# Graph attention kernel: placement one-hots built one group ahead, aggregation put first in TensorE's group

## The chip, the cores and the metric

One NeuronCore of one Trainium2 chip. The metric is the device time of one execution in microseconds (us), as the median of the runs shown; lower is better.

## What is computed

The reference is one transformer-like layer over a graph: x becomes x + GNN(norm x) + linear attention(norm x), and then x + mixture of experts(norm x), for 3125 nodes of 256 features. The part around the change is the graph attention over 53125 edges, which come sorted by their target:

```python
mod_k = K[src] + 0.2 * rel_w[edge_relations][:, None, :]
scores = jnp.einsum('ehd,ehd->eh', Q[dst], mod_k) / D ** 0.5      # 4 heads of 64
ex = jnp.exp(scores - segment_max(scores, dst)[dst])
w = ex / segment_sum(ex, dst)[dst]
agg = segment_sum(w[:, :, None] * V[src], dst)
```

Everything else (layer norms, projections, linear attention, top-2 routing and experts) is untouched.

## The kernel before, in words

The kernel runs in phases: projections (to about 205 us), edges (`phase_edges`, about 205 to 884 us), combination, routing, experts, end. Only the edge phase concerns us.

Edges are handled in blocks of 128. A step is two blocks (256 edges) that all point into one block of 128 nodes; the code numbers steps by p. A group, numbered `G_`, is 4 blocks, so two steps, and a chunk, numbered c, is 4 groups (g = 0 to 3). There are 29 chunks and 116 groups. Every engine has its own list of instructions, written out in Python in the order in which it runs; semaphores tie the lists together, and nothing reorders them.

All engines walk through rounds i = 0 to 30 of four groups. In round i three chunks are in work at once:

- chunk i is **scored**. POOL (GpSimd) has gathered the rows of K and V of its edges into the ring `KV` with one indirect DMA for each block (L572). VectorE compares the edge's target and relation with an iota to make the one-hots `PT` and `OT` of the group after (`onehots`, L743 and L744). TensorE multiplies them with the relation table (`relations`, into `ps_u`) and the queries (`queries`, one for each step, into `ps_qe`). VectorE adds `ps_u` to K (`modify`, L754), multiplies by `ps_qe` (`multiply`, L761, one for each step) and sums over a head (`reduce`, L767).
- chunk i-1 goes through the **softmax**: the scores are turned on TensorE (`turn_scores` in g = 0, `turn_ends` in g = 1, `turn_carries` in g = 2, `turn_weights` in g = 3) and VectorE runs the segment maxima in between: `run_forward` and `run_backward` (SF, SB) in g = 0, `carry` and `carried` (EC, EZ, CR) in g = 1, two `carry_in` and `differences` (SM, SD) in g = 2, `first_rows` and `factors` (OH, LR) in g = 3.
- chunk i-2 is **summed**. ScalarE weighs the V rows (`weigh`, L587; in the last two chunks VectorE does every other step). VectorE makes the placement one-hots `PM` of a whole group (`place`, L772): `PM[edge, node] = (iota == DC[edge])`. TensorE multiplies the weighed V rows by `PM` (`aggregate`, L677) and adds the block's old sums (`add_sums`, L683), and ScalarE copies the result back into `ACC` (`keep_sums`, L595).

`PM` has two buffers, and `place(p)` waits until the `aggregate` two groups back is done (`s_pw`); `aggregate(p)` waits for `s_pm` (the placement) and `s_wv` (the weighed rows). In VectorE's group the order is: one-hots of the next group, `modify`, `place`, first `multiply`, second `multiply`, `reduce`, with the softmax instructions strewn in. In TensorE's group it is: a turn of the softmax, `relations`, `add_sums(p-1)`, `queries`, `aggregate(p)`, `add_sums(p)`, `queries`, (`turn_weights`), `aggregate(p+1)`.

Of the kernel before, what the change touches and what calls it, by code (L numbers as in the profile page):

```python
# [74 lines left out]
def wait(eng, sem, count):  # L75

    if isinstance(count, int) and count <= 0:
        return
    eng.wait_ge(sem, count)
# [8 lines left out]
def load_values(nc, engine, ap, high):  # L88

    return nc.values_load_multi_w_load_instructions(ap, engines=(engine,), min_val=0, max_val=high,  # L90
                                                    skip_runtime_bounds_check_because="the step list holds node blocks only")[1]
# [421 lines left out]
def phase_edges(nc, sem, T, d):  # L513
# [9 lines left out]
    NG = NCH * CG  # L523
    NP = NCH * CP
# [6 lines left out]
    def on_vector(p):  # L531
        return p >= VP and p % 2 == 1
# [4 lines left out]
    with nc.Block() as block:  # L537
# [103 lines left out]
        @block.tensor  # L641
        def _(pe):
            def relations(G_):
                h = G_ % 2
                pe.wait_ge(s_oh, 2 * G_ + 2)
                wait(pe, s_ku, G_ - 1)
                for k in range(G):
                    for n in range(3):
                        m = pe.matmul(T["ps_u"][:, h, k * D:(k + 1) * D], T["OT"][:, h, k * P:(k + 1) * P], T["rel3"][:, n, :],  # L649
                                      start=(n == 0), stop=(n == 2))  # L650
                m.then_inc(s_u, 1)

            def queries(p, at):
                h = p // 2 % 2
                wait(pe, s_mu, p - 2)
                for k in range(2):
                    for n in range(3):
                        m = pe.matmul(T["ps_qe"][:, p % 3, k, :], T["PT"][:, h, (p % 2 * 2 + k) * P:(p % 2 * 2 + k + 1) * P],  # L658
                                      T["Q3"][:, bass.ds(at + n * C, C)], start=(n == 0), stop=(n == 2))
                m.then_inc(s_qe, 1)  # L660

            def rows(G_):
                return load_values(nc, mybir.EngineType.PE, T["qRow"][0:1, 2 * G_:2 * G_ + 2], (NT - 1) * 3 * C)

            def blocks(p):
                return load_values(nc, mybir.EngineType.PE, T["aRow"][0:1, p:p + 2], (NT - 1) * A)

            def aggregate(p):
                c, x = divmod(p, CP)
                pe.wait_ge(s_pm, p // 2 + 1)  # L670
                if on_vector(p):
                    pe.wait_ge(s_wd, (p - VP) // 2 + 1)
                else:
                    pe.wait_ge(s_wv, p + 1 if p < VP else VP + (p - VP) // 2 + 1)
                wait(pe, s_acc, p - 1)
                for k in range(2):
                    m = pe.matmul(T["ps_o"][:, p % 2, 0:A], PM[:, p // 2 % 2, p % 2 * 2 + k, :], kv[:, c % KR, 2 * x + k, C:KVW], start=(k == 0), stop=False)  # L677
                m.then_inc(s_pw, 1)

            def add_sums(p, at):  # L680
                wait(pe, s_acc, p)
                pe.wait_ge(s_rs, p // CP + 1)
                pe.matmul(T["ps_o"][:, p % 2, 0:A], T["ident"][:, :], ACC[:, bass.ds(at, A)], start=False, stop=True).then_inc(s_o, 1)  # L683

            def turn_scores(c):
                pe.wait_ge(s_sc, (c + 1) * CG)
                wait(pe, s_w, 2 * c)
                pe.transpose(ps_s[0:B, 0:P], S[:, c % 2, :], T["ident"][:, :]).then_inc(s_t1, 1)

            def turn_ends(c):  # L690
                pe.wait_ge(s_sm, c * SMV + 2)
                pe.transpose(ps_s[0:1, P:P + B], T["SB"][:, P - 1:P], T["ident"][0:B, 0:B])
                pe.transpose(ps_s[0:1, P + B:P + 2 * B], T["SB"][:, 0:1], T["ident"][0:B, 0:B]).then_inc(s_t2, 1)

            def turn_carries(c):
                pe.wait_ge(s_sm, c * SMV + 7)
                pe.transpose(ps_s[0:B, 256:257], T["CR"][0:1, 0, :], T["ident"][0:1, 0:1])
                pe.transpose(ps_s[0:B, 257:258], T["CR"][0:1, 1, :], T["ident"][0:1, 0:1]).then_inc(s_t3, 1)

            def turn_weights(c):  # L700
                pe.wait_ge(s_ex, c + 1)
                pe.transpose(ps_s[:, 264:264 + B], T["SE"][:, 0:P], T["ident"][0:B, 0:B])
                pe.wait_ge(s_lr, c + 1)
                pe.matmul(ps_s[:, 258:258 + H], T["LR"][:, :], T["ident"][0:H, 0:H], start=True, stop=True).then_inc(s_t4, 1)
            at = rows(0)
            relations(0)
            queries(0, at[0])
            queries(1, at[1])
            for i in range(NCH + 2):
                for g in range(CG):  # L710
                    p = (i - 2) * CP + 2 * g
                    G_ = i * CG + g + 1
                    if 1 <= i <= NCH:
                        (turn_scores, turn_ends, turn_carries, lambda c: None)[g](i - 1)
                    if G_ < NG:
                        at = rows(G_)
                        relations(G_)
                    if p >= 1:
                        add_sums(p - 1, before)
                    if G_ < NG:  # L720
                        queries(2 * G_, at[0])
                    if p >= 0:
                        to = blocks(p)
                        aggregate(p)
                        add_sums(p, to[0])
                        before = to[1]
                    if G_ < NG:
                        queries(2 * G_ + 1, at[1])
                    if 1 <= i <= NCH and g == 3:
                        turn_weights(i - 1)  # L730
                    if p >= 0:
                        aggregate(p + 1)
            add_sums(NP - 1, before)

        @block.vector
        def _(v):
# [26 lines left out]
            def reduce(G_):  # L763
                c, g = divmod(G_, CG)
                v.wait_ge(s_mu, 2 * G_ + 2)
                wait(v, s_t1, c - 1)
                v.tensor_reduce(S[:, c % 2, g * G * H:(g + 1) * G * H].rearrange("p (s h) -> p s h", h=H),  # L767
                                keys(G_).rearrange("p s (h d) -> p s h d", h=H), AX.X, ALU.add).then_inc(s_sc, 1)

            def place(p):  # L770
                wait(v, s_pw, p - 2)
                v.tensor_tensor(PM[:, p // 2 % 2, :, :], T["iota_f"][:, :].unsqueeze(1).broadcast_to([P, G, P]),  # L772
                                T["DC"][:, 2 * p:2 * p + G].unsqueeze(2).broadcast_to([P, G, P]), ALU.is_equal).then_inc(s_pm, 1)
# [81 lines left out]
            for i in range(NCH + 2):  # L855
                for g in range(CG):
                    G_ = i * CG + g
                    p = (i - 2) * CP + 2 * g
                    c = i - 1
                    scored, softmax, summed = G_ < NG, 1 <= i <= NCH, i >= 2  # L860
                    if G_ + 1 < NG:
                        onehots(G_ + 1)
                    if softmax and g == 3:
                        first_rows(c)
                    if scored:
                        modify(G_)
                    if softmax and g == 2:
                        carry_in(c, 0)
                    if softmax and g == 3:
                        factors(c)  # L870
                    if summed:
                        place(p)
                    if softmax and g == 0:
                        run_forward(c)
                    if softmax and g == 2:
                        carry_in(c, 1)
                    if scored:
                        multiply(2 * G_)
                    if softmax and g == 2:
                        differences(c)  # L880
                    if summed and on_vector(p + 1):
                        weigh(p + 1)
                    if scored:
                        multiply(2 * G_ + 1)
                    if summed and g == 0:
                        rescale(i - 2)
                    if softmax and g == 0:
                        run_backward(c)
                    if softmax and g == 1:
                        carry(c)  # L890
                    if scored:
                        reduce(G_)
                    if softmax and g == 1:
                        carried(c)

# [776 lines left out]
```

## Time and profile before

| | us |
|---|---|
| median of 3 runs (1359.99 to 1361.61) | 1360.5 |
| the profiled execution, its own time | 1360.95 |
| its span in the profile | 1359.1 |
| VectorE (DVE) busy over the span | 939.8 (69%) |
| TensorE (PE) busy | 1123.6 (83%) |
| ScalarE (ACT) busy | 816.7 (60%) |
| POOL busy | 776.2 (57%) |

The shares are averages over all phases and say little about one of them. How to read it: first the table by stretches of the edge phase (how busy each engine is there), then the table of waits (who stands still, and for whom), then the timeline of single instructions. A record of an instruction often starts some 0.07 us before its forerunner's ends, so what an instruction costs is the distance from its start to the next one's start, not its duration.

### The profile page before, as it was taken

Reading aid. Unit: us, or ns where it says so; the run is one execution under the profiler, and the core shown is the slowest. Engines: PE = TensorE matmul, PEld = TensorE weight load, DVE = VectorE, ACT = ScalarE, POOL = GpSimd, SP = SyncE. Lnnn points to the kernel's source line nnn. Section 1 sums busy time; section 2 is a strip of 40 time slices with the busy share of each in tenths; the row PEclk is TensorE's granted clock in tenths of the full one; section 3 lists DMA queues with packets and bytes.
Section 4 is the critical chain, followed back from the end, with each engine's and each line's share of the span. In section 5 each row is a group of like instructions: output and inputs, shape, how many; then the busy total and the mean of one; then the engine's idle time right before and its main releaser. Section 6 shows DMA issues by size and latency. Waiting matters only on the chain. (4 is left out here: it accounts for less than half of the span.)

```text
span 1359.1 us, 26561 instructions
## 1 busy us (share of the span) xinstructions
PE 1123.6 (83%) x7285; PEld 867.0 (64%) x7286; DVE 939.8 (69%) x2100; ACT 816.7 (60%) x2868; POOL 776.2 (57%) x853
## 2 busy tenths in 40 slices
PE   5999926899999999999999998756775589999950
PEld 3777724566666666666666666545653379999940
DVE  7676327999999999999999999346563812122215
ACT  3444300588888888888888888512342066776630
POOL 4666347777777777777777774033220644554520
PEclk9999966799999999999999999989985789999985
DMA  7332358888788888878778775092101822221218
GB/s 224 114 104 98 109 111 254 237 236 230 234 227 235 227 236 233 232 231 231 231 232 233 229 234 155 0 328 81 39 20 61 257 59 70 66 69 66 69 37 281
DMA packets 132710, 225.06 MB, mean 166 GB/s; under 512 B 23555, under 2 KB 89098, under 8 KB 132594
## 3 DMA queue, kind: packets, MB, share of 16 engines
q0 software_dynamic: 43456, 138.49, 34.9%
q1 hardware_dynamic: 89138, 85.16, 20.7%
q8 instruction: 56, 0.92, 0.3%
q14 instruction: 60, 0.49, 0.1%
HBM read 191.18 MB, written 32.40 MB: 165 GB/s over the span
## 5 line engine op out<-in xcount | busy, mean ns | idle before, releaser
L572 POOL DMA_INDIRECT KV<-kv,ixs x464 | 494.4, 1065 | 142.6 <-issue 139.6
L587 ACT ACTIVATE KV<-KV,WS 128x65 f32<-128x65 f32 x1792 | 453.6, 337 | 22.5 <-ACT RR L613 17.0
L677 PE MATMUL ps_o<-KV,PM 128*128 128x260 f32 x928 | 256.2, 399 | 25.8 <-DVE PM L772 12.8
L677 PEld LDWEIGHTS ps_o<-KV,PM 128*128 128x128 f32 x928 | 158.7, 190 | 73.8 <-DVE PM L772 29.5
L658 PE MATMUL ps_qe<-Q,PT 128*128 x1392 | 199.6, 282 | 5.2 <-DVE KV L761 5.2
L658 PEld LDWEIGHTS ps_qe<-Q,PT 128*128 128x128 bf16 x1392 | 138.7, 100 | 55.2 <-issue 8.5
L683 PE MATMUL ps_o<-ACC,ident 128*128 x464 | 154.2, 414 | 0.0
L761 DVE TENSOR_TENSOR KV<-KV,ps_qe 128x512 f32<-128x512 f32 x232 | 148.4, 667 | 0.2
L754 DVE TENSOR_TENSOR KV<-KV,ps_u 128x1024 f32<-128x1024 f32 x116 | 139.6, 1204 | 6.9 <-DMA KV<-kv,ixs 6.9
L1491 DVE TENSOR_TENSOR YG<-ps_y,B 128x256 f32<-128x256 f32 x56 | 23.8, 425 | 170.1 <-PE ps_y L1465 170.1
L767 DVE TENSOR_REDUCE S<-KV 128x16 f32<-128x1024 f32 x116 | 139.4, 1202 | 2.0
L595 ACT COPY ACC<-ps_o 128x260 f32 x232 | 85.0, 366 | 55.7 <-PE ps_o L683 54.8
L1408 ACT ACTIVATE HT<-ps_h,WB 128x128 f32<-128x128 f32 x224 | 82.2, 367 | 60.2 <-PE ps_h L1449 47.2
L1449 PE MATMUL ps_h<-XT,WB 128*128 128x128 f32 x896 | 115.2, 282 | 0.0
L1449 PEld LDWEIGHTS ps_h<-XT,WB 128*128 128x128 f32 x896 | 105.7, 194 | 5.3 <-issue 2.2
L1379 POOL DMA_INDIRECT ytab<-YG,DX x56 | 55.3, 987 | 93.2 <-issue 83.4
L1465 PE MATMUL ps_y<-W,HT 128*128 x448 | 105.8, 380 | 0.0
L683 PEld LDWEIGHTS ps_o<-ACC,ident 128*128 128x128 f32 x464 | 76.8, 189 | 21.1 <-issue 9.3
L649 PE MATMUL ps_u<-rel,OT 64*128 64x64 bf16 x1392 | 62.0, 194 | 32.3 <-DVE OT L744 29.3
L649 PEld LDWEIGHTS ps_u<-rel,OT 64*128 64x128 bf16 x1392 | 50.6, 97 | 56.5 <-DVE OT L744 45.3
L1465 PEld LDWEIGHTS ps_y<-W,HT 128*128 128x128 f32 x448 | 81.0, 191 | 8.6
L772 DVE TENSOR_TENSOR PM<-iota_f,DC 128x512 f32<-128x512 f32 x116 | 78.1, 674 | 3.7 <-PE ps_o L677 3.7
(300 smaller groups left out, 1685.3 us busy)
## 6 DMA issues: line engine op xcount, KB each, us to landing
dlb<-dl_rows SPq DMA_DIRECT2D x116, 128.0 KB
W<-in_f_W_dram SPq DMA_DIRECT2D x16, 512.0 KB, 6.2
tyb<-ty_rows SPq DMA_DIRECT2D x116, 64.0 KB
KV<-kv,ixs POOLq DMA_INDIRECT x464, 4.3
kv<-kvb SPq DMA_DIRECT2D x25, 258.0 KB, 2.3
xs_rows<-xs SPq DMA_DIRECT2D x25, 256.0 KB, 2.4
YF<-ytab SPq DMA_DIRECT2D x8, 640.0 KB, 9.2
VB<-kv SPq DMA_DIRECT2D x5, 650.0 KB, 9.1
```

Source lines behind the costliest of these rows:

```text
L572: pool.indirect_dma_start(kv[:, c % KR, n, :], None, d["kv"], bass.IndirectOffsetOnAxis(ap=T["ixs"][:, c % KR, n:n + 1], axis=0)).then_inc ...
L587: m = a.activation(part, part, ACT.Copy, scale=W[:, c % 2, s * H + h:s * H + h + 1])
L595: a.copy(ACC[:, bass.ds(at, A)], T["ps_o"][:, p % 2, 0:A]).then_inc(s_acc, 1)
L649: m = pe.matmul(T["ps_u"][:, h, k * D:(k + 1) * D], T["OT"][:, h, k * P:(k + 1) * P], T["rel3"][:, n, :], start=(n == 0), stop=(n == 2))
L658: m = pe.matmul(T["ps_qe"][:, p % 3, k, :], T["PT"][:, h, (p % 2 * 2 + k) * P:(p % 2 * 2 + k + 1) * P], T["Q3"][:, bass.ds(at + n * C, C)] ...
L677: m = pe.matmul(T["ps_o"][:, p % 2, 0:A], PM[:, p // 2 % 2, p % 2 * 2 + k, :], kv[:, c % KR, 2 * x + k, C:KVW], start=(k == 0), stop=False)
L683: pe.matmul(T["ps_o"][:, p % 2, 0:A], T["ident"][:, :], ACC[:, bass.ds(at, A)], start=False, stop=True).then_inc(s_o, 1)
L754: v.tensor_tensor(k, k, T["ps_u"][:, G_ % 2, 0:G * D].rearrange("p (s d) -> p s d", s=G).unsqueeze(2).broadcast_to([P, G, H, D]), ALU.add) ...
L761: v.tensor_tensor(k, k, T["ps_qe"][:, p % 3, :, :], ALU.mult).then_inc(s_mu, 1)
L767: v.tensor_reduce(S[:, c % 2, g * G * H:(g + 1) * G * H].rearrange("p (s h) -> p s h", h=H), keys(G_).rearrange("p s (h d) -> p s h d", h= ...
L1449: r = pe.matmul(T["ps_h"][:, m, 0:SLOTS], WB[:, u % 2, k * HID + m * P:k * HID + (m + 1) * P], XT[:, u % 2, k, :], start=(k == 0), stop=(k ...
L1465: r = pe.matmul(T["ps_y2"][:, (u % YB) * HB + w, 0:C], HT[:, u % 2, m, w * P:(w + 1) * P], T["W2"][:, bass.ds(at + m * C, C)], start=(m == ...
```

## The change

`place` moves from the middle of VectorE's group, where it made the placements of the step pair p in the group in which they are used, to the end of the group before. It now follows `reduce`, and comes ahead of `carried` in g = 1 and ahead of the next group's `onehots`. On TensorE the group now begins (after the softmax turn) with `add_sums(p-1)` and `aggregate(p)`; `relations` and the first `queries` come behind them, then `add_sums(p)`, `aggregate(p+1)`, and the second `queries` last. No instruction is added or removed, and buffers stay as they are.

```diff
                         (turn_scores, turn_ends, turn_carries, lambda c: None)[g](i - 1)
+                    if p >= 1:
+                        add_sums(p - 1, before)
+                    if p >= 0:
+                        to = blocks(p)
+                        aggregate(p)
                     if G_ < NG:
                         at = rows(G_)
                         relations(G_)
-                    if p >= 1:
-                        add_sums(p - 1, before)
-                    if G_ < NG:
                         queries(2 * G_, at[0])
                     if p >= 0:
-                        to = blocks(p)
-                        aggregate(p)
                         add_sums(p, to[0])
                         before = to[1]
-                    if G_ < NG:
-                        queries(2 * G_ + 1, at[1])
                     if 1 <= i <= NCH and g == 3:
                         turn_weights(i - 1)
                     if p >= 0:
                         aggregate(p + 1)
+                    if G_ < NG:
+                        queries(2 * G_ + 1, at[1])
...
                         factors(c)
-                    if summed:
-                        place(p)
                     if softmax and g == 0:
...
                         reduce(G_)
+                    if -2 <= p < NP - 2:
+                        place(p + 2)
                     if softmax and g == 1:
                         carried(c)
```

VectorE, from `modify` of g = 1 to the next group's one-hots, in a middle round. Before:

```order
L754 TENSOR_TENSOR KV<-KV,ps_u 128x4x256
L772 TENSOR_TENSOR PM<-iota_f,DC 128x512
L761 TENSOR_TENSOR KV<-KV,ps_qe 128x2x256 x2
L816 SCALAR_TENSOR_TENSOR EC<-ET,EZ 1x72
L817 SCALAR_TENSOR_TENSOR EC<-ET,EZ 1x72
L767 TENSOR_REDUCE S<-KV 128x16
L824 COPY EZ<-EC 1x4
L825 TENSOR_TENSOR CR<-EC,ET 1x4x16
L826 TENSOR_TENSOR CR<-EC,ET 1x4x16
L743 TENSOR_SCALAR PT<-dlb,iota_p 128x512
L744 TENSOR_SCALAR OT<-tyb,iota_p 64x512
```

and the same engine with the change, from the same `multiply` on, into g = 2:

```order
L761 TENSOR_TENSOR KV<-KV,ps_qe 128x2x256 x2
L816 SCALAR_TENSOR_TENSOR EC<-ET,EZ 1x72
L817 SCALAR_TENSOR_TENSOR EC<-ET,EZ 1x72
L767 TENSOR_REDUCE S<-KV 128x16
L772 TENSOR_TENSOR PM<-iota_f,DC 128x512
L824 COPY EZ<-EC 1x4
L825 TENSOR_TENSOR CR<-EC,ET 1x4x16
L826 TENSOR_TENSOR CR<-EC,ET 1x4x16
L743 TENSOR_SCALAR PT<-dlb,iota_p 128x512
L744 TENSOR_SCALAR OT<-tyb,iota_p 64x512
L754 TENSOR_TENSOR KV<-KV,ps_u 128x4x256
L835 SCALAR_TENSOR_TENSOR SM<-BR,ps_s,SB 64x128
```

The placement no longer stands between L754 and L761, and it now stands shortly ahead of the one-hots L743 and L744 (next to them in every group but this one, where `carried` lies between).

TensorE, the group g = 1 of a middle round (L649 relations, L658 queries, L677 aggregate, L683 add_sums). Before:

```order
L649 MATMUL ps_u<-rel,OT 128x64 x12
L683 ISA
L683 MATMUL ps_o<-ACC,ident 128x260
L658 ISA
L658 MATMUL ps_qe<-Q,PT 128x256
L658 ISA
L658 MATMUL ps_qe<-Q,PT 128x256
L658 ISA
L658 MATMUL ps_qe<-Q,PT 128x256 x4
L90 TENSOR_LOAD aRow
L677 MATMUL ps_o<-KV,PM 128x260 x2
```

and with the change:

```order
L692 MATMUL ps_s<-ident,SB 1x64
L693 MATMUL ps_s<-ident,SB 1x64
L683 ISA
L683 MATMUL ps_o<-ACC,ident 128x260
L90 TENSOR_LOAD aRow
L677 MATMUL ps_o<-KV,PM 128x260 x2
L90 TENSOR_LOAD qRow
L649 MATMUL ps_u<-rel,OT 128x64 x12
```

The work that needs the fresh one-hots `OT` now stands behind an `add_sums` and an `aggregate` that need nothing made in VectorE's same group.

## Rows read from the trace of the kernel before

**Rows 1.** Table by stretches, 500 to 600 us; the header names the columns

```profile
core 0: us, PE busy (x) PEld busy (x) DVE busy (x) ACT busy (x) POOL busy (x), PEclk, DMA share, GB/s
500.00:600.00 100.00, 94.21 (x691) 68.53 (x690) 99.69 (x195) 87.28 (x353) 77.75 (x74) 1.00 0.82 232
```

**Rows 2.** Table of waits, TensorE, 300 to 820 us: us in total, times, longest

```profile
PE ps_u L649 <- DVE OT L744: 15.0, 33, 0.6
PE ps_o L677 <- DVE PM L772: 8.6, 23, 0.4
```

**Rows 3.** Timeline, VectorE, the target one-hots PT; start, us, engine, line, operation

```profile
521.72 0.49 DVE L743 TENSOR_SCALAR PT<-dlb,iota_p 128x512 bf16<-128x512 bf16 x1
...
527.24 0.41 DVE L743 TENSOR_SCALAR PT<-dlb,iota_p 128x512 bf16<-128x512 bf16 x1
...
532.79 0.56 DVE L743 TENSOR_SCALAR PT<-dlb,iota_p 128x512 bf16<-128x512 bf16 x1
...
538.16 0.35 DVE L743 TENSOR_SCALAR PT<-dlb,iota_p 128x512 bf16<-128x512 bf16 x1
...
543.78 0.49 DVE L743 TENSOR_SCALAR PT<-dlb,iota_p 128x512 bf16<-128x512 bf16 x1
```

**Rows 4.** Timeline, VectorE: modify ahead of multiply, and modify ahead of the placement

```profile
234.83 1.22 DVE L754 TENSOR_TENSOR KV<-KV,ps_u 128x1024 f32<-128x1024 f32 x1 [0.17 <-DMA KV<-kv,ixs]
236.09 1.29 DVE L761 TENSOR_TENSOR KV<-KV,ps_qe 128x512 f32<-128x512 f32 x2
...
256.29 1.20 DVE L754 TENSOR_TENSOR KV<-KV,ps_u 128x1024 f32<-128x1024 f32 x1
257.42 0.67 DVE L772 TENSOR_TENSOR PM<-iota_f,DC 128x512 f32<-128x512 f32 x1
```

**Rows 5.** Timeline, VectorE, group 6: the two carry_in with nothing between

```profile
241.33 0.34 DVE L835 SCALAR_TENSOR_TENSOR SM<-BR,ps_s,SB 64x128 f32<-64x128 bf16 x1
241.71 0.35 DVE L835 SCALAR_TENSOR_TENSOR SM<-BR,ps_s,SM 64x128 f32<-64x128 bf16 x1
241.98 0.67 DVE L761 TENSOR_TENSOR KV<-KV,ps_qe 128x512 f32<-128x512 f32 x1
```

**Rows 6.** Timeline, POOL and VectorE: one-hots that start inside a gather

```profile
289.38 0.95 POOL L572 DMA_INDIRECT KV<-kv,ixs  x1 [0.31 <-issue]
...
289.88 0.57 DVE L743 TENSOR_SCALAR PT<-dlb,iota_p 128x512 bf16<-128x512 bf16 x1
```

**Rows 7.** Timeline, POOL: a gather that starts inside the placement at 257.42

```profile
257.50 1.43 POOL L572 DMA_INDIRECT KV<-kv,ixs  x1 [0.31 <-DVE KV L754]
```

**Rows 8.** Timeline, VectorE and POOL: a gather that starts inside CR, PT and OT behind

```profile
261.71 0.25 DVE L826 TENSOR_TENSOR CR<-EC,ET 1x64 f32<-1x64 f32 x1
261.85 0.33 DVE L743 TENSOR_SCALAR PT<-dlb,iota_p 128x512 bf16<-128x512 bf16 x1
262.11 0.34 DVE L744 TENSOR_SCALAR OT<-tyb,iota_p 64x512 bf16<-64x512 bf16 x1
...
261.75 1.53 POOL L572 DMA_INDIRECT KV<-kv,ixs  x1 [0.30 <-issue]
```

**Rows 9.** Timeline: last gather of a group and the modify that reads it, early and in the middle

```profile
245.92 0.95 POOL L572 DMA_INDIRECT KV<-kv,ixs  x1 [0.30 <-issue]
...
250.74 1.22 DVE L754 TENSOR_TENSOR KV<-KV,ps_u 128x1024 f32<-128x1024 f32 x1 [0.38 <-DMA KV<-kv,ixs]
...
516.12 0.95 POOL L572 DMA_INDIRECT KV<-kv,ixs  x1 [0.30 <-issue]
...
522.39 1.20 DVE L754 TENSOR_TENSOR KV<-KV,ps_u 128x1024 f32<-128x1024 f32 x1
```

**Rows 10.** Timeline, TensorE: relations and queries of one group

```profile
517.72 0.51 PE L649 MATMUL ps_u<-rel,OT 64*128 64x64 bf16 x12
...
518.70 0.82 PE L658 MATMUL ps_qe<-Q,PT 128*128 x6
```

**Rows 11.** Timeline, TensorE, the last scored group's first aggregate

```profile
844.31 1.14 PE L677 MATMUL ps_o<-KV,PM 128*128 128x260 f32 x4 [1.60 <-DVE PM L772]
```

## The prediction

> **What bounds the kernel now.** I read three views, in this order. First the table by stretches [rows 1]: in the middle of the edge phase VectorE is busy 99.69 of 100 us, TensorE 94.21, ScalarE 87.28, POOL 77.75, and the granted clock is 1.00, the upper of TensorE's two levels, so no clock is to be won. Then the table of waits [rows 2]: TensorE does wait for what the change touches, 15.0 us for the relation one-hots and 8.6 us for the placements in 520 us, together nearly 1.0 us in each of the 23.5 chunks that fit there. That is what the new order removes. But a wait on an engine that is not the last one costs nothing, and VectorE has no row of waiting at all in that stretch. So the third view is the timeline of VectorE, start to start: a chunk takes 22.06 us, from the one-hots at 521.72 to the same ones at 543.78 [rows 3]. TensorE's 23.6 us are therefore no term of the sum. Only what shortens or lengthens VectorE's own chunk is.
>
> **What the change does to VectorE's chunk.** The same instructions run; their neighbours change, and that has a price in three places.
>
> One. In g = 1 the placement stood between `modify` and the first `multiply`, which reads what `modify` wrote. Where the two stood next to each other, the starts are 236.09 - 234.83 = 1.26 us apart; with the placement behind `modify` they are 257.42 - 256.29 = 1.13 [rows 4]. The cover goes, and 0.13 us is added. In g = 0 and g = 3 a softmax instruction (SF, LR) is left between, in g = 2 two of them, so nothing is added there.
>
> Two. In g = 2 the placement stood between the two `carry_in`, of which the second reads the first. Side by side they start 0.38 us apart, while the one after follows its forerunner, on which it doesn't depend, after 0.27 [rows 5]: 0.11 us added. Together 0.24 us a chunk.
>
> Three, a gain that the diff doesn't show. The one-hots PT last 0.49, 0.41, 0.56 and 0.35 us in the four groups of a chunk [rows 3], the same from chunk to chunk. The shortest is 0.35 and early rows go to 0.33; I take 0.34 as the work itself, and (0.15 + 0.07 + 0.22 + 0.01) = 0.45 us a chunk as time lost. The loss has a place: PT starts 0.50 us into a gather of POOL and ends 0.12 after it, 290.45 against 290.33 [rows 6]. POOL loses by VectorE too: the gather that starts at 257.50 inside the placement (257.42 to 258.09) lasts 1.43 us instead of 0.95 [rows 7], that is, it ends 0.84 after the placement, as if begun 0.11 before its end. The closest picture of the new order is the one where POOL's gather begins inside CR and the two one-hots follow closely [rows 8]: there PT and OT run at 0.33 and 0.34, unstretched, and it is the gather that waits until OT's end (262.45 + 0.83 = 263.28, its end). With the change every pair of one-hots comes behind a placement, which like CR reads two tensors of SBUF. POOL needs 4 x (0.95 + 0.30) = 5.0 us for a group and VectorE 5.5, so POOL gains on VectorE in every group until a placement catches it; then PT runs free. So I take the whole 0.45 as won. Bounds of this term: 0 (POOL stays in a phase where PT starts half-way into a gather) and 0.45, and I stand at the upper end since the rows that look like the new order are [rows 8].
>
> The sum for a chunk is 0.13 + 0.11 - 0.45 = -0.21 us, so 21.85 for 22.06. Placement and softmax both run in 27 rounds; the first of them still waits for gathers, so 26 count: -5.5 us.
>
> The Trainium skill, "SBUF — State Buffer", section "SBUF: two separate sides", has a rule for this: VectorE and GpSimd share one pair of ports as an exclusive lock, and whoever starts first holds it for its whole instruction. For the stretched PT the trace agrees (0.57 us, ended by the gather's end). By the letter of it a gather under way would hold the one-hots for up to 0.95 us in the new order as well, and a chunk could lose the 0.45 again or more. This rule speaks against the gain, and is the ground of rival B below.
>
> **TensorE and ScalarE.** TensorE's group loses its waits for OT and PM, together 1.0 us a chunk, all of it slack. A new wait can arise in g = 0: `aggregate` needs rows that ScalarE can only weigh once the softmax weights have come from `turn_weights`, and relations (0.51) and queries (0.82) [rows 10] no longer stand between. That is at most 1.3 us a chunk. The cover is TensorE's idle time, 5.8 us in 100 [rows 1], so 1.3 us a chunk; I cost it at nothing, and at 0 to 0.3 if the cover is short. What is queued behind this wait is the next relations and queries. VectorE needs those only in its next group: relations ready at 518.23 are read by the `modify` at 522.39, and queries ready at 519.52 by the `multiply` 1.13 us behind it [rows 4, 9, 10], so each may be 4 us late for free, more than the `aggregate` and `add_sums` that they now stand behind and the new wait make together. The second `queries`, now last in the group, are needed one `multiply` later still. SP's loads of the next rows hang on the one-hots, which keep their place in the group. Each `place` runs one group earlier and waits for an `aggregate` of the group before, done by then. POOL's queue has nothing moved.
>
> **The ends.** In the last scored group TensorE stands 1.60 us for the placement [rows 11]; the new order has it ready. Between 0 and 1.60 us can be won; ScalarE is weighing the rows for the same product at that time, so I take 0.4. After that, weighing paces everything and the order is as before. Early, the first placement falls into a group end followed by a wait for gathers (0.38 us before the `modify` at 250.74 [rows 9]); I take 0.
>
> Total -5.9 us on the profiled execution's own 1360.95, so 1355.1; the median of the runs is 0.45 lower, and the forecast is **1355** us in round numbers. What a measurement of this kernel can tell from no change is about 0.2%, 2.7 us.
>
> **Rivals.**
>
> A, slower: the gathers become the bound. A placement alone holds a gather to about 0.1 us before its own end; with PT and OT behind it, the hold reaches from the placement's start over PM 0.60 (0.67 less the overlap of 0.07), PT 0.26 and OT 0.34, less 0.12: 1.1 us [rows 7, 8], more in g = 1 and g = 2, where CR and OH join the row; I take 1.2. POOL's group is then 5.0 plus a hold of 0 to 1.2 us. As long as the mean hold is below 5.5 - 5.0 = 0.45, VectorE sets the pace; above it, VectorE waits in `modify`. For a random phase the mean is 0.6, a group 5.6, a chunk 22.5 or 0.45 more than now: +12 us, 1373. If each gather is caught at the placement's start, a group is 6.2 and 104 groups add 80 us. For it: the hold is twice as long as now, and the reserve is small: a gather's landing takes 250.74 - 246.87 = 3.9 us after its record ends, and the lead in the middle is 522.39 - 517.07 = 5.3 [rows 9], 1.4 us to spare. Against it: a lead, once there, grows whenever VectorE is the slower of the two, and then POOL is only held for the difference. Chance 0.17.
>
> B, slower: a gather that began just before the placement holds the one-hots behind it, as in [rows 6], and the stretch of PT stays at its 0.45 in another phase. It decides if POOL's gather has passed its start before VectorE's placement takes the memory. The sum becomes +0.24 x 26 = +6.2, less 0.4: 1367. Chance 0.09.
>
> C, no change: a third to half of the 0.45 stays, or TensorE's new wait in g = 0 eats 0.1 to 0.2 us of each chunk. -0.05 a chunk, 1359. Chance 0.20.
>
> D, faster by far: VectorE's 99.7% hides waits inside its records, and TensorE's 1.0 us of waiting a chunk is really on the path: -26 us, 1335. Against it stands that VectorE's steps add up to its chunk with nothing left over. Chance 0.03.
>
> My forecast has 0.51. Its own range is 1349 (both dependence costs absent, the gain whole: -0.45 x 26 = -11.7) to 1358. The range for everything must leave out no more than 2 in 10: it goes from 1349 up to 1373, over B and to A's middle value, and leaves out D and the worse half of A. Faster is the forecast and D, 0.54; within 0.2% is C, 0.20; slower are A and B, 0.26.
>
> **What would show it.** Right: PT near 0.34 us in all four groups; the start of `modify` to that of `multiply` 1.26 in g = 1 and the two `carry_in` 0.38 apart; no row of TensorE waiting for PM, hardly one for OT; gathers of more than 1 us, ended by OT's end, about one a group; a chunk of 21.85. Wrong: `modify` with idle time ended by the gathers (rival A), PT still at 0.4 to 0.6 (B), `multiply` waiting for `ps_qe` or SF for `turn_scores` (TensorE became late, C).

## The result and the profile after

| | before | with the change |
|---|---|---|
| median of 4 runs each, us | 1360.24 (1359.47 to 1361.61) | 1387.72 (1386.67 to 1389.86) |
| ratio, 95% interval | | 1.0203 [1.0185, 1.0221] |
| span of the profiled execution, us | 1359.1 | 1384.9 |

The change makes the kernel 2.0% slower, 27.5 us. The forecast was 1355, its range ended at 1373, and most of the chance stood on faster. Both the sign and the range were wrong.

The same three views, in the same order. First the table by stretches of the kernel with the change, 500 to 600 us (columns as in [rows 1]):

```profile
500.00:600.00 100.00, 88.45 (x653) 63.56 (x651) 93.91 (x179) 82.49 (x334) 71.77 (x69) 1.00 0.78 220
```

Every engine is less busy than in [rows 1]: VectorE 93.91 for 99.69, TensorE 88.45 for 94.21. The granted clock is 1.00 as before. When all engines lose share together, no single one of them has become the bound; they wait for each other in turn. Then the table of waits, 300 to 820 us (us in total, times, longest):

```profile
PE ps_o L677 <- issue: 58.3, 89, 1.2
ACT ACC L595 <- PE ps_o L683: 57.7, 76, 1.1
POOL KV L572 <- PE ps_o L683: 46.4, 46, 1.7
DVE SF L805 <- PE ps_s L688: 24.7, 22, 1.5
```

The two rows of [rows 2] are gone, as foreseen. In their place TensorE stands 58.3 us ahead of `aggregate` (L677), 89 times, which is once in every group, and 58.3 / 520 x 23.12 = 2.6 us a chunk. ScalarE stands 57.7 us ahead of `keep_sums` (L595) for `add_sums` (L683); the kernel before has the same row, but shorter:

```profile
ACT ACC L595 <- PE ps_o L683: 35.8, 88, 0.6
```

VectorE, which had no waiting row, stands 24.7 us in `run_forward` (SF) for the turned scores (L688), 1.1 us in each of 22 chunks. "issue" ahead of L677 means that the view found no releaser; the timeline below shows that `weigh` (L587) ends just before.

VectorE's own instructions did what the forecast said. Its timeline with the change:

```profile
452.41 0.35 DVE L743 TENSOR_SCALAR PT<-dlb,iota_p 128x512 bf16<-128x512 bf16 x1
453.13 1.20 DVE L754 TENSOR_TENSOR KV<-KV,ps_u 128x1024 f32<-128x1024 f32 x1
...
457.56 0.35 DVE L743 TENSOR_SCALAR PT<-dlb,iota_p 128x512 bf16<-128x512 bf16 x1
...
460.39 0.41 DVE L805 TENSOR_TENSOR_SCAN SF<-BR,ps_s 64x128 f32<-64x128 bf16 x1 [1.10 <-PE ps_s L688]
...
464.35 0.34 DVE L743 TENSOR_SCALAR PT<-dlb,iota_p 128x512 bf16<-128x512 bf16 x1
464.87 1.20 DVE L754 TENSOR_TENSOR KV<-KV,ps_u 128x1024 f32<-128x1024 f32 x1
466.11 1.28 DVE L761 TENSOR_TENSOR KV<-KV,ps_qe 128x512 f32<-128x512 f32 x2
...
469.87 0.34 DVE L743 TENSOR_SCALAR PT<-dlb,iota_p 128x512 bf16<-128x512 bf16 x1
...
476.25 1.20 DVE L754 TENSOR_TENSOR KV<-KV,ps_u 128x1024 f32<-128x1024 f32 x1
```

PT lasts 0.34 to 0.35 in all four groups, where [rows 3] has 0.35 to 0.56, and `modify` to `multiply` in g = 1 is 466.11 - 464.87 = 1.24. Yet the chunk is 476.25 - 453.13 = 23.12 us for 22.06: the 1.10 of waiting stands in the middle of it. Of 23.12 us VectorE is idle (100 - 93.91)% = 1.41, so its work is 21.71, a little less than the 21.85 that I forecast for a chunk without waits. The loss, 1.06 us a chunk by 26 = 27.6 us, is all waiting.

Where the wait comes from is seen when one follows a single step around TensorE and ScalarE. The timeline with the change, from the `aggregate` of step p to that of step p+2, with the `aggregate` of step p-2 on top:

```profile
455.16 1.12 PE L677 MATMUL ps_o<-KV,PM 128*128 128x260 f32 x4 [0.93 <-issue]
...
461.46 1.11 PE L677 MATMUL ps_o<-KV,PM 128*128 128x260 f32 x4 [0.74 <-issue]
...
462.51 0.52 PE L649 MATMUL ps_u<-rel,OT 64*128 64x64 bf16 x12
462.96 0.83 PE L658 MATMUL ps_qe<-Q,PT 128*128 x6
463.63 0.60 PE L683 MATMUL ps_o<-ACC,ident 128*128 x2
...
464.35 0.38 ACT L595 COPY ACC<-ps_o 128x260 f32 x1 [0.80 <-PE ps_o L683]
...
464.90 2.03 ACT L587 ACTIVATE KV<-KV,WS 128x65 f32<-128x65 f32 x8 [0.18 <-issue]
...
467.03 1.11 PE L677 MATMUL ps_o<-KV,PM 128*128 128x260 f32 x4 [0.43 <-issue]
...
472.62 1.11 PE L677 MATMUL ps_o<-KV,PM 128*128 128x260 f32 x4 [0.50 <-issue]
```

and in the kernel before:

```profile
519.56 1.11 PE L677 MATMUL ps_o<-KV,PM 128*128 128x260 f32 x4
...
520.60 0.70 PE L683 MATMUL ps_o<-ACC,ident 128*128 x2
...
521.55 0.36 ACT L595 COPY ACC<-ps_o 128x260 f32 x1
...
521.96 2.03 ACT L587 ACTIVATE KV<-KV,WS 128x65 f32<-128x65 f32 x8
...
524.54 1.04 PE L677 MATMUL ps_o<-KV,PM 128*128 128x260 f32 x4
```

It is a ring: `aggregate(p)`, `add_sums(p)`, `keep_sums(p)`, then `weigh(p+2)`, which stands behind `keep_sums(p)` in ScalarE's list, then `aggregate(p+2)`. Before, `add_sums` starts 1.04 us behind `aggregate`, and there is slack at the ring's end: `weigh` ends at 523.99, and `aggregate` starts 0.55 us later, behind TensorE's other work. Now `relations` and the first `queries` of the next group are between `aggregate` and `add_sums`, which starts 2.17 us behind. A round takes 467.03 - 461.46 = 5.57 us, 472.62 - 467.03 = 5.59, and the one from g = 3 to g = 0, in which `turn_weights` and the copies of WS and RR stand as well, 6.30 (455.16 to 461.46). The last `aggregate` of the chunk, at 478.29, follows 5.67 behind 472.62. That the four rounds make 23.13 us, a chunk, proves nothing by itself: four rounds of any list do. What counts is that nowhere in this ring is there slack: in all four rounds each link starts at most 0.6 us behind the end of its forerunner, on whichever engine that is, and none of its links waits for VectorE. In the round from g = 3 to g = 0 two ways end together, `keep_sums` at 458.43 and `turn_weights` at 458.45, and ScalarE's copy of WS starts at 458.48; that round would hardly be shorter with `add_sums` further ahead, the other three would. The place where VectorE pays is SF: TensorE works without a pause from the `aggregate` at 455.16, which the ring holds back, through the second `queries`, now ahead of `turn_scores`, to the end of `turn_scores` at 460.28, and SF starts at 460.39.

### The profile page after: what moved, and what is told of

Same layout as the page of the kernel before. It is cut to its first block and busy times, and to the rows that moved or that the text cites. A ratio compares the mean times of both kernels' runs of the same rounds, so it can differ in the third digit from the quotient of the medians.

```text
span 1384.9 us, 26561 instructions
## 1 busy us (share of the span) xinstructions
PE 1111.8 (80%) x7285; PEld 855.1 (62%) x7286; DVE 938.0 (68%) x2100; ACT 817.2 (59%) x2868; POOL 764.4 (55%) x853
## 5 line engine op out<-in xcount | busy, mean ns | idle before, releaser
L572 POOL DMA_INDIRECT KV<-kv,ixs x464 | 480.9, 1036 | 180.1 <-issue 128.2
L587 ACT ACTIVATE KV<-KV,WS 128x65 f32<-128x65 f32 x1792 | 453.7, 336 | 28.1 <-ACT RR L613 16.9
L677 PE MATMUL ps_o<-KV,PM 128*128 128x260 f32 x928 | 253.8, 396 | 82.6 <-issue 74.0
L677 PEld LDWEIGHTS ps_o<-KV,PM 128*128 128x128 f32 x928 | 165.0, 190 | 145.8 <-issue 123.0
L658 PE MATMUL ps_qe<-Q,PT 128*128 x1392 | 200.2, 283 | 3.6 <-DVE KV L761 3.6
L658 PEld LDWEIGHTS ps_qe<-Q,PT 128*128 128x128 bf16 x1392 | 129.9, 100 | 42.1 <-issue 6.1
L761 DVE TENSOR_TENSOR KV<-KV,ps_qe 128x512 f32<-128x512 f32 x232 | 149.1, 671 | 1.8 <-PE ps_qe L658 0.6
L683 PE MATMUL ps_o<-ACC,ident 128*128 x464 | 146.3, 397 | 0.0
L754 DVE TENSOR_TENSOR KV<-KV,ps_u 128x1024 f32<-128x1024 f32 x116 | 139.7, 1204 | 4.6 <-DMA KV<-kv,ixs 4.5
L595 ACT COPY ACC<-ps_o 128x260 f32 x232 | 84.6, 364 | 97.3 <-PE ps_o L683 85.4
L649 PEld LDWEIGHTS ps_u<-rel,OT 64*128 64x128 bf16 x1392 | 48.9, 97 | 53.2 <-issue 36.9
L683 PEld LDWEIGHTS ps_o<-ACC,ident 128*128 128x128 f32 x464 | 70.6, 191 | 7.2 <-issue 0.6
L649 PE MATMUL ps_u<-rel,OT 64*128 64x64 bf16 x1392 | 62.9, 194 | 13.9 <-DVE OT L744 13.9
```

Source lines behind the costliest of these rows:

```text
L572: pool.indirect_dma_start(kv[:, c % KR, n, :], None, d["kv"], bass.IndirectOffsetOnAxis(ap=T["ixs"][:, c % KR, n:n + 1], axis=0)).then_inc ...
L587: m = a.activation(part, part, ACT.Copy, scale=W[:, c % 2, s * H + h:s * H + h + 1])
L595: a.copy(ACC[:, bass.ds(at, A)], T["ps_o"][:, p % 2, 0:A]).then_inc(s_acc, 1)
L754: v.tensor_tensor(k, k, T["ps_u"][:, G_ % 2, 0:G * D].rearrange("p (s d) -> p s d", s=G).unsqueeze(2).broadcast_to([P, G, H, D]), ALU.add) ...
L761: v.tensor_tensor(k, k, T["ps_qe"][:, p % 3, :, :], ALU.mult).then_inc(s_mu, 1)
```

## Experiments

The theory, **ring**: the loss comes from what stands between `aggregate(p)` and `add_sums(p)`, and goes with its length. Rivals: the placement's new place (beside the one-hots and POOL's gathers) costs; or it costs as such that TensorE's work for VectorE stands behind an `aggregate`.

The 18 runs fell into two kinds of sessions. In one, the kernel before took 1361 us, as in the result. In the others it took 1468 to 1481, and ratios there are measured against that. The expectations call it another kind of chip; but the recorded chip number is the same for one session at 1481 and for the one at 1361, so whether it is the chip is not known. The granted clock differs too: over 300 to 820 us it is 1.00 in every profile of the 1361-us kind (before, after, before_q, v_sh40), and in the other 0.98 for the kernel before, 0.90 to 0.92 for VectorE's part alone, and 0.86 to 0.89 for sums_next3, rel_between and the full change.

### VectorE's part alone: v_only, and again

```diff
-                    if summed:
-                        place(p)
...
                         reduce(G_)
+                    if -2 <= p < NP - 2:
+                        place(p + 2)
```

TensorE's list is that of the kernel before.

> VectorE's part alone: place one group ahead and behind reduce; TensorE's order as before. Theory 1 (the slowdown is a ring between TensorE and ScalarE that only TensorE's new order makes: aggregate, relations and queries, add_sums, keep_sums, weigh, aggregate two steps on): this kernel has no such ring, VectorE sets the pace, PT lasts 0.34 us in every group, a chunk takes 21.85 us and the kernel 1354 to 1356. Theory 2 (the placement ahead of the one-hots is what costs, through POOL's gathers or VectorE's own steps): most of the 27 us is here, 1375 or more, with modify waiting for gathers.

> VectorE's part alone. Theory 1: a chunk of 21.85 us, PT 0.34 us in every group, 1354 to 1356 where the kernel before takes 1360. Theory 2: 1375 or more, with modify waiting for gathers.

> VectorE's part alone, TensorE's list as in the kernel before. Theory ring and port gain: on a chip where the kernel before takes 1360 about 1355; on one where it takes 1475 again 1.045. Rival (the placement at the group's end has a price of its own on every chip): 1.02 or more on the first kind of chip too.

Measured: 1538.64 us, 1.046 [1.043, 1.049]; 1536.80, 1.042 [1.036, 1.047]; 1534.42, 1.041 [1.035, 1.048], all in sessions of the second kind (1475-us sessions from here on). The forecast for it was missed: a clear loss where none, or a gain, was expected. What it is made of is taken up below, with its counterpart in a 1361-us session.

### TensorE's part alone: t_only, and the placement in its old spot

t_only is the change with `place(p)` back where it was; ahead_mid has `place(p + 2)`, one group ahead as in the change, but in the old spot between `modify` and `multiply`.

> TensorE's part alone: its new order, with place in its old spot, made in the group that uses it. Theory 1: the ring is whole, 1386 to 1392, no faster than the full change; a placement that is ready only some 1.8 us behind modify is about as late as the weighed rows. Theory 2: about 1360, since the placement is where it was.

> The full change, but place(p + 2) stands between factors and run_forward or multiply, its old spot in the group, still a group ahead. Theory 1: VectorE isn't the bound, so its neighbours don't matter: 1385 to 1390, as the full change. Theory 2 (placement, one-hots and gathers in a row are the cost): the row is broken up, so back to 1360 or less.

Measured: t_only 1606.06, 1.092 [1.088, 1.095]; ahead_mid 1609.28, 1.093 [1.088, 1.098]. The full change in such sessions is 1.096 to 1.100 (below). So where `place` stands makes little difference once TensorE has its new order; TensorE's order carries the large part.

### add_sums directly behind aggregate: sums_next, four times

```diff
                         aggregate(p)
+                        add_sums(p, to[0])
+                        before = to[1]
                     if G_ < NG:
                         at = rows(G_)
                         relations(G_)
                         queries(2 * G_, at[0])
-                    if p >= 0:
-                        add_sums(p, to[0])
-                        before = to[1]
```

Everything else is the full change, the `aggregate` ahead of `relations` included.

> The full change, but add_sums(p) directly behind aggregate(p), ahead of relations and queries. Theory 1: relations and queries (1.1 us from start to start) leave the ring, which falls from 5.6 to about 4.5 us a group, below VectorE's 5.46; a chunk is 21.85 to 22.0 and the kernel 1354 to 1358. If only the hand-over of the softmax weights in g = 0 were the cause (6.3 us in that group), it would stay above 1375: the path from turn_weights to the first aggregate is unchanged.

> The full change with add_sums(p) directly behind aggregate(p). Theory 1: the ring falls from 5.6 to about 4.5 us a group, below VectorE's 5.46, and the kernel takes 1354 to 1358 where the kernel before takes 1360. If only the hand-over of the softmax weights in g = 0 were the cause, it stays above 1375.

> The full change with add_sums(p) directly behind aggregate(p). Theory ring: the 1.0 us a chunk that the change loses on the first chip is gone, so on a chip where the kernel before takes 1360 about 1355 (0.995 to 1.00); on one where it takes 1475, 1540 as before (1.045). Rival (the placement at the group's end has a price of its own on every chip): 1.02 or more on the first kind of chip too.

> The full change with add_sums(p) directly behind aggregate(p). If this is a chip where the kernel before takes 1360: theory ring, the time of VectorE's part alone, 0.990 to 1.000 (a chunk of 21.8 to 22.0 us, VectorE over 99% busy). Rival (TensorE's new order costs as such, with relations and queries behind an aggregate): 1.01 or more. If it takes 1475: 1.045 as before.

Measured, all in 1475-us sessions: 1540.98, 1539.79, 1544.30 and 1540.35 us, ratios 1.048, 1.043, 1.046 and 1.046 (the widest interval 1.037 to 1.052). It is within 0.7% of the time of v_only in the same sessions. So there, that `relations` and `queries` stand behind an `aggregate` costs next to nothing; that they stand ahead of `add_sums` costs 5%. The clock does not make that difference, since sums_next3 and full3 both have 0.86. One caution: these kernels do not stand still alike (below). VectorE waits 58.9 us in `modify` for something outside the core in sums_next3, 40.7 in full3 and not at all in v_only3, in 300 to 820 us, so the near equality with v_only may in part be chance.

### The full change on the same ground, and the kernel before

> The full change once more, beside the kernel before on one chip, since the first four kernels ran where the kernel before itself took 1470 us and ScalarE stood for 4 to 6 us at a time on something that came from outside the core. Theory 1 (the ring between TensorE and ScalarE): 1385 to 1390 where the kernel before takes 1360; every chunk 23.1 us; VectorE waits 1.1 us a chunk for turn_scores. Theory 2 (placement beside the one-hots): the same time.

> The full change again, beside the other three on the same chip: 1388 (1.02) on a chip where the kernel before takes 1360, 1615 (1.09) where it takes 1475. It is the mark that tells which of the two kinds of chip these four ran on.

> The kernel before, unchanged, for its profile on the chip where it takes 1476 us. If ScalarE's standstills of 5 to 6 us, ended from outside the core, are the chip's and not the change's, they are here too, about one in 29 us, and the chunk takes some 26 us instead of 22.1. If they belong to the new orders, ScalarE has none of them here and something else makes the 1476.

Measured: full2 1621.18, 1.096 [1.089, 1.104]; full3 1620.70, 1.100 [1.094, 1.105]; before_here 1489.07 beside 1480.83 for the same kernel, one execution each.

### Half of it between them: rel_between, twice

```diff
                         relations(G_)
-                        queries(2 * G_, at[0])
                     if p >= 0:
                         add_sums(p, to[0])
                         before = to[1]
+                    if G_ < NG:
+                        queries(2 * G_, at[0])
```

> The full change, but of the two pieces that it put between aggregate(p) and add_sums(p) only relations stays there; the first queries comes behind add_sums(p). Theory ring (what lies between the two lengthens aggregate -> add_sums -> keep_sums -> weigh -> next aggregate by its own time): relations is 0.45 us of the 1.2, so the ring of 5.58 us becomes about 4.8 within a chunk and 5.5 from g = 3 to g = 0, below or at VectorE's 5.4 a group, so the time is that of sums_next. On a chip where the kernel before takes 1360: about 1355, ratio 1.00; on one where it takes 1475: a ratio of 1.04 to 1.05. Rival: it is enough that TensorE's work for VectorE stands behind an aggregate, whatever is between aggregate and add_sums: then as the full change, 1388 (1.02) or 1610 (1.09).

> relations alone between aggregate(p) and add_sums(p), the first queries behind. If this is a chip where the kernel before takes 1360: theory ring, the four rings of a chunk are 0.82 us shorter each than in the full change, 3.3 us of its 23.1, so VectorE bounds again: 0.990 to 1.003. Rival (it is enough that they stand behind an aggregate): 1.02. If it takes 1475: 1.065 as before.

Measured: 1580.23, 1.065 [1.054, 1.076], and 1572.41, 1.072 [1.068, 1.076]. Neither the time of sums_next, which I expected since the ring should have fallen below VectorE's pace, nor that of the full change, which the rival wanted: it lies half-way. The dose shows in the waits as well. TensorE ahead of `aggregate`, 300 to 820 us, in sums_next3:

```profile
PE ps_o L677 <- issue: 13.1, 23, 1.5
PE ps_o L677 <- ACT KV L587: 1.6, 1, 1.6
```

in rel_between:

```profile
PE ps_o L677 <- issue: 22.3, 32, 1.6
PE ps_o L677 <- ACT KV L587: 20.6, 15, 1.6
```

and in full3:

```profile
PE ps_o L677 <- ACT KV L587: 41.9, 28, 1.7
PE ps_o L677 <- issue: 26.3, 28, 1.6
```

14.7, 42.9 and 68.2 us in the same stretch, with nothing, with `relations`, and with `relations` and `queries` between `aggregate` and `add_sums`; the median chunk, from `modify` to `modify`, is 28.6, 29.8 and 31.2 us. In these sessions the time grows with what stands between the two, and from the first piece on. Why the ring costs more there than in the others (5%, where the full change is 2.6% above v_sh40 in the other kind) is not shown; one reading is that the rounds are stretched by stalls from outside (below) and have no slack to give.

### Only the ring, in the kernel before: before_q

```diff
-                    if G_ < NG:
-                        queries(2 * G_, at[0])
                     if p >= 0:
                         to = blocks(p)
                         aggregate(p)
+                    if G_ < NG:
+                        queries(2 * G_, at[0])
+                    if p >= 0:
                         add_sums(p, to[0])
```

> The kernel before with one piece moved: the first queries of a group goes from ahead of aggregate(p) to between aggregate(p) and add_sums(p). Theory ring: the way aggregate -> add_sums -> keep_sums -> weigh -> aggregate becomes 0.8 us longer and nothing else changes, so the kernel gets slower by what rel_between and full3 differ by on this chip, 1.02 to 1.04. Rival (the loss comes from relations and queries being late for VectorE, or from add_sums(p-1) and aggregate(p) standing ahead of them): 1.00, since in this kernel they stand where they stood or 1.1 us later.

Measured, in the 1361-us session: 1371.10 for 1361.05, 1.007 [1.005, 1.009]. The sign is the one expected; the size, taken from the other sessions, was too large. The timeline from g = 3 to g = 0:

```profile
541.16 1.14 PE L677 MATMUL ps_o<-KV,PM 128*128 128x260 f32 x4 [1.03 <-DVE PM L773]
...
542.79 0.60 PE L683 MATMUL ps_o<-ACC,ident 128*128 x2
...
543.51 0.38 ACT L595 COPY ACC<-ps_o 128x260 f32 x1 [0.97 <-PE ps_o L683]
...
544.19 0.38 PE L704 MATMUL ps_s<-ident,LR 4*128 4x4 f32 x2
...
544.61 0.21 ACT L612 COPY WS<-ps_s 128x64 f32<-128x64 f32 x1 [0.71 <-PE ps_s L704]
...
545.46 2.03 ACT L587 ACTIVATE KV<-KV,WS 128x65 f32<-128x65 f32 x8 [0.58 <-ACT RR L613]
...
547.59 0.68 PE L677 MATMUL ps_o<-KV,PM 128*128 128x260 f32 x2 [0.70 <-ACT KV L587]
...
547.95 0.43 DVE L788 SCALAR_TENSOR_TENSOR ACC<-RR,ACC 128x260 f32 x1 [0.51 <-ACT ACC L595]
```

This round is 6.43 us, and the chunk 22.60 (from the `aggregate` at 524.99 to that at 547.59), 0.5 more than before. One piece out of two gives a third of the full loss. But the rows show another way than the ring. `keep_sums` ends at 543.89, and ScalarE's copy of WS starts 0.72 us later, for `turn_weights` (L704): the way over `add_sums` and `keep_sums` has slack in this round. What is late is `turn_weights`. `aggregate`, moved up by a `queries`, first waits 1.03 us for the placement, since this kernel makes it in the same group, and the `queries` and all behind it start that much later. VectorE pays at `rescale` (L788), which waits for ScalarE's `keep_sums`, 0.5 us a chunk (11.6 us, 24 times), the whole difference. This loop, from `place` over TensorE and ScalarE back to `rescale`, runs through VectorE; the ring of the full change does not. So before_q shows that TensorE's order alone can cost VectorE time by way of ScalarE, and is no test of the ring.

### VectorE's part in the 1361-us session: v_sh40, v_sh80, before_sh40

```diff
+            for n in range(40):
+                a.copy(T["pad"][:, n:n + 1], T["SRC"][:, 0:1])
             for i in range(NCH + 2):
```

These add 40 (in v_sh80 80) tiny copies to ScalarE's list, ahead of its first `weigh`, where it is idle; v_sh40 and v_sh80 are v_only with them, before_sh40 the kernel before with them. They were meant to move the stalls that ScalarE shows in the 1475-us sessions.

> The kernel before with 40 tiny copies (128 x 1, into a tile nobody reads) added to ScalarE's list at a time when it is idle, ahead of its first weigh. Theory L (the stalls of ScalarE on this chip come with the place in its own list of instructions): they move to other groups of the chunk and the time changes, by up to 3% in either direction. Theory D (they come with what the DMA engines carry at that time): nothing moves, 1.00.

> v_only3 with the same 40 copies. Theory L: the one stall of 5.5 us a chunk leaves the place just ahead of exponents, and the ratio leaves 1.041, down to between 0.99 and 1.03. Theory D: 1.041 again, stall in the same place.

> v_only3 with 80 copies. Theory L: a ratio that differs from that of v_sh40 and of v_only3. Theory D: 1.041 again.

Measured: before_sh40 1360.14, 0.9997 [0.9986, 1.0008]; v_sh40 1351.98, 0.9941 [0.9922, 0.9961]; v_sh80 1351.41, 0.9925 [0.9901, 0.9949]. There were no such stalls when these ran, so about them the three say nothing. They say something better: the copies cost nothing, so v_sh40 and v_sh80 are a clean measurement of VectorE's part, a gain of 8 to 10 us. The rows of v_sh40 (here L745 is PT, L756 `modify`, L837 `carry_in`):

```profile
500.00:600.00 100.00, 93.92 (x694) 69.27 (x693) 99.35 (x195) 85.89 (x353) 74.68 (x75) 1.00 0.83 237
```

```profile
502.05 0.33 DVE L745 TENSOR_SCALAR PT<-dlb,iota_p 128x512 bf16<-128x512 bf16 x1
502.57 1.20 DVE L756 TENSOR_TENSOR KV<-KV,ps_u 128x1024 f32<-128x1024 f32 x1
503.71 0.34 DVE L837 SCALAR_TENSOR_TENSOR SM<-BR,ps_s,SB 64x128 f32<-64x128 bf16 x1
504.08 0.35 DVE L837 SCALAR_TENSOR_TENSOR SM<-BR,ps_s,SM 64x128 f32<-64x128 bf16 x1
...
507.65 0.35 DVE L745 TENSOR_SCALAR PT<-dlb,iota_p 128x512 bf16<-128x512 bf16 x1
...
512.80 0.35 DVE L745 TENSOR_SCALAR PT<-dlb,iota_p 128x512 bf16<-128x512 bf16 x1
...
518.38 0.34 DVE L745 TENSOR_SCALAR PT<-dlb,iota_p 128x512 bf16<-128x512 bf16 x1
...
524.38 1.20 DVE L756 TENSOR_TENSOR KV<-KV,ps_u 128x1024 f32<-128x1024 f32 x1
```

The chunk is 524.38 - 502.57 = 21.81 us; the forecast said 21.85. VectorE is busy 99.35 of 100 us, PT is 0.33 to 0.35 in every group, and `carry_in` to `carry_in` 0.37. v_sh80 and v_sh40 are the fastest kernels of this study; v_only without the copies was not run in such a session. Against them the full change, at 1387.7, loses 36 us; beside the copies it differs from them in TensorE's order alone.

## Why the prediction was wrong, step by step

- **VectorE's chunk: right.** It forecast +0.13, +0.11 and -0.45, 21.85 us in all. With VectorE's part alone 21.81 was measured, with PT unstretched and the two `carry_in` 0.37 us apart; `modify` to `multiply`, read with the full change, is 1.24. For the whole kernel it forecast -5.9 us, and v_sh40 and v_sh80 gave -9.1 and -9.6. The chunks are 26 x (22.06 - 21.81) = 6.5 us of that; the rest is at the ends or within the intervals.
- **TensorE and ScalarE: this step failed.** It read: "A new wait can arise in g = 0", "at most 1.3 us a chunk. The cover is TensorE's idle time", "I cost it at nothing". It asked what `aggregate` waits for, and never what `add_sums` waits for. The change put `relations` and `queries` ahead of `add_sums(p)` in all four groups, 2.17 - 1.04 = 1.1 us in each round of the ring. Measured were 2.6 us of waits a chunk ahead of `aggregate`, twice the cover that I named, and they stand in all four groups, not in g = 0 alone; but cover was the wrong measure anyway. Idle time on TensorE hides TensorE's lateness only if nothing that it makes comes back to it. Here it comes back through ScalarE every group.
- **The slack for VectorE's inputs: right for what it named, and incomplete.** `modify` and `multiply` wait for `ps_u` and `ps_qe` nowhere in the table of waits of the change in the 1360-us session (in full3 they do, 9.8 us each). `turn_scores` was not on my list, though the second `queries` had moved ahead of it.
- **Rival A (gathers) and rival B (stretched PT): false in the 1360-us sessions.** VectorE never waits for a gather in the middle of the phase there, with the change or with VectorE's part alone, and PT is at most 0.35 us with VectorE's part alone and above 0.36 in 3 of 90 with the change. In the other sessions it does stand in `modify`, for something outside the core; what that is, a gather or not, is not known. Two readings of the prediction were loose. The worst case of A, a group of 6.2 us, adds (6.2 - 5.515) x 104 = 71 us, not 80. And the trace agreed with the Trainium skill ("SBUF — State Buffer", section "SBUF: two separate sides") only in part when that says that whoever starts first holds the shared ports for its whole instruction: a PT held until the gather's end at 290.33 would have needed its own 0.34 us after it, and ended 0.12 after. With the change a gather starts at 463.52 and the placement 0.23 us into it, at 463.75; the placement takes its usual 0.67 us, PT and OT behind it 0.34 each, and it is the gather that takes 1.73 instead of 0.95. By that rule the placement would have waited. So the condition that I had named for B came true in g = 1, and the cost did not.
- **Rival C: the right sign of being wrong, the mechanism in part, the size too small.** It had TensorE's new wait, in g = 0, at 0.1 to 0.2 us a chunk; the loss against VectorE's own 21.8 is 1.3, from all four groups. The sign that I had named for it, SF waiting for `turn_scores`, is the row that appeared.
- **Rival D: false.** The 1.0 us of TensorE's waits that went was slack, as argued.

What supports the ring: in the trace of the change its four rounds run without slack and without VectorE, with TensorE waiting for weighed rows in every group; that v_sh40, which differs in TensorE's order, loses nothing; and the dose in the second kind of session. What is not shown: neither sums_next nor rel_between ever ran in a 1361-us session, so that the full change with only `add_sums` put back would be as fast as v_sh40 there is argued, not measured. The part that the second `queries` ahead of `turn_scores` has in VectorE's 1.1 us was not tried by itself.

## To carry to other kernels

Before an instruction is moved on an engine that isn't the bound, follow each result that it is put ahead of around the other engines until it comes back to the same list. What the period of the bound leaves over that round's time is the slack, and idle share is not. Two things moved together should be costed, and tried, apart: here one gained 0.6 to 0.75% and the other took back about four times that.

## What the runs showed of the hardware that was not expected

In the 1475-us sessions engines stand still for something outside the core, which the table of waits writes as "remote". In 300 to 1000 us the kernel before (before_here) has

```profile
ACT ACC L595 <- remote: 103.6, 52, 4.5
POOL KV L572 <- remote: 63.7, 49, 1.9
```

and v_only3 has

```profile
ACT ACC L595 <- remote: 133.3, 26, 6.0
POOL KV L572 <- remote: 7.0, 3, 2.4
```

In sums_next3 and full3 VectorE has one as well, in `modify` (L753, L754), 81.1 and 50.2 us; v_only3 and before_here have next to none there. In the profiled executions of the 1360-us sessions (before, after, before_q, v_sh40) no such row exists in that stretch. In v_only3 it is one stall a chunk, always at the same place:

```profile
516.83 0.38 ACT L595 COPY ACC<-ps_o 128x260 f32 x1 [5.48 <-remote]
517.10 0.31 ACT L606 ACTIVATE SE<-SD 64x129 f32<-64x129 f32 x1
517.34 1.23 PE L683 MATMUL ps_o<-ACC,ident 128*128 x2 [4.11 <-ACT ACC L595]
517.54 0.34 DVE L851 SCALAR_TENSOR_TENSOR LR<-OH,SE 4x128 f32<-4x128 f32 x1 [3.56 <-ACT SE L606]
```

The `add_sums` that this `keep_sums` needs had started at 509.84 for 0.60 us, and ScalarE's last `weigh` ended at 509.32 + 2.02 = 511.34, so ScalarE stood 5.5 us with its work ready, and TensorE 4.1 and VectorE 3.6 us behind it. The kernel before has two shorter stalls of ScalarE in most chunks, 1.7 and 1.9 us, elsewhere in the chunk. The difference in ScalarE's stalls, 5.5 against 3.6 us, is 1.9 of the 2.6 us that v_only's median chunk is longer there (28.1 for 25.5), so I hold it for most of the reason that v_only is 4% slower in those sessions and 0.6 to 0.75% faster in the other; that is argued, not shown. The clock may have a share in the rest: behind the stall of 4.11 us the granted clock is 0.50 from 517.3 to 519.0 us, the lower of TensorE's two levels, and the `add_sums` there lasts 1.23 us for the 0.60 of the one at 509.84. After before_here's shorter stalls it stays at 1.00 (500 to 600 us), where v_only3 has 0.93. What ScalarE waits for there (its own instructions would be one candidate), and why the two kinds of sessions differ, stays open. A ratio from such a session is worth something only between kernels that stall alike.
